# A two-layer decoder on one core: moved feed-forward layers, a reordered junction, and an output projection and bias rows in rounded products

## The reference, cut to what matters

```python
# layer 0, self-attention: ctx is 448 x 2048, out_w is 2048 x 256
return ctx @ out_w + out_b
# layer 0, cross-attention, and layer 1, summary
delta = _nan_clean(ctx @ Wo.T + bo)
proj = jnp.einsum('btd,ed->bte', states, W_out) + b_out
# layer 1, feed-forward: W1 is 1024 x 256, W2 is 256 x 1024, SCALE = 0.1
h = jnp.einsum('bsd,fd->bsf', x, W1)
q = jnp.clip(jnp.round(h / SCALE), -32768, 32767)
return jnp.einsum('bsf,df->bsd', jax.nn.gelu(q * SCALE), W2)
```

## Time and profile before

| quantity | value |
|---|---|
| time, median of 3 runs | 526.32 us (525.9 to 528.05) |
| time of the profiled execution | 528.47 us |
| its span, first to last instruction | 526.7 us |
| around the span | 1.77 us |
| mean granted clock of TensorE | 0.987 |
| TensorE busy | 497.3 us, 94% |
| VectorE busy | 352.1 us, 67% |
| ScalarE busy | 312.9 us, 59% |

### The profile page before, as it was taken

One profiled execution on the slowest core, in us unless ns is written; L12 is line 12 of the kernel. 1 busy time (PEld: TensorE's weight loads), 2 busy tenths in 40 slices (PEclk: granted clock), 3 DMA queues, 4 the chain that ended last, 5 costly groups with the idle time before them and its releaser, 6 DMA issues.

```text
span 526.7 us, 16180 instructions
## 1 busy us (share of the span) xinstructions
PE 497.3 (94%) x7004; PEld 405.7 (77%) x7010; DVE 352.1 (67%) x784; ACT 312.9 (59%) x550; POOL 4.2 (1%) x14
## 2 busy tenths in 40 slices
PE   8999999998889999999999998999999899888897
PEld 7898888886678888877878876888878678645455
DVE  5656767876456764674856686855778764798971
ACT  5657677446256656567566667568467755363252
POOL 1000000000100000000000000000000000000000
PEclk9999999999989999999999999999999999899999
DMA  6366551203202111111211101210111100000000
GB/s 201 110 232 194 189 154 42 60 12 142 88 1 64 59 42 41 41 41 41 75 35 46 27 30 36 67 37 22 40 41 42 51 2 2 1 1 9 1 0 19
DMA packets 12232, 30.84 MB, mean 59 GB/s; under 512 B 1665, under 2 KB 4866, under 8 KB 11394
## 3 DMA queue, kind: packets, MB, share of 16 engines
q1 hardware_dynamic: 11714, 29.07, 17.4%
q0 software_dynamic: 192, 0.51, 0.3%
q10 hardware_dynamic: 256, 0.23, 0.1%
HBM read 29.35 MB, written 0.46 MB: 57 GB/s over the span
## 4 chain that ended last, share of the span: by engine, by line
PE 66%; DVE 17%; ACT 11%; issue 4%; DMA 1%; SPq 0%; DVEq 0%; ACTq 0%
PE psb L1334 10%; PE psb L1324 10%; PE psa L1390 7%; PE psa L1246 6%; PE psb L1408 5%; PE pst L1267 4%; PE psa L1259 3%; PE psb L1297 3%; PE psa L1277 2%; PE pst L1558 2%; ACT shared L590 2%; ACT smem L590 1%; DVE smem L910 1%; PE psb L1288 1%; PE psa L1558 1%
## 5 line engine op out<-in xcount | busy, mean ns | idle before, releaser
L1334 PE MATMUL psb<-wkv,cx 128*125 128x256 f32 x576 | 81.5, 291 | 3.4 <-ACT kx L430 3.4
L1324 PE MATMUL psb<-cx,wkv 128*128 128x500 f32 x276 | 75.4, 409 | 4.1 <-ACT vmem L437 4.1
L1334 PEld LDWEIGHTS psb<-wkv,cx 128*125 128x125 f32 x576 | 72.0, 188 | 7.3 <-ACT kx L430 5.8
L437 ACT ACTIVATE vmem<-psb 125x512 f32<-125x512 f32 x48 | 28.6, 596 | 62.0 <-PE psb L1334 62.0
L1324 PEld LDWEIGHTS psb<-cx,wkv 128*128 128x128 f32 x276 | 48.9, 190 | 16.4 <-ACT vmem L437 4.7
L910 DVE TENSOR_SCALAR shared<-shared,top 125x896 f32<-125x896 f32 x48 | 30.8, 684 | 41.7 <-ACT shared L590 41.5
L1390 PE MATMUL psa<-qb,kx 32*125 32x112 f32 x1536 | 55.6, 282 | 1.4 <-ACT vmem L437 0.8
L1390 PEld LDWEIGHTS psa<-qb,kx 32*125 32x125 f32 x1536 | 47.1, 186 | 9.7 <-issue 4.9
L910 DVE TENSOR_SCALAR smem<-smem,top 125x896 f32<-125x896 f32 x48 | 30.8, 683 | 28.5 <-ACT smem L590 28.5
L590 ACT ACTIVATE shared<-psa 125x1792 f32<-125x1792 f32 x24 | 40.0, 1668 | 13.4 <-PE psa L1390 13.3
L590 ACT ACTIVATE smem<-psa 125x1792 f32<-125x1792 f32 x24 | 40.0, 1666 | 12.0 <-PE psa L1390 11.9
(11 more groups left out here) (311 smaller groups left out, 809.2 us busy)
## 6 DMA issues: line engine op xcount, KB each, us to landing
ring<-ctx_t_dram SPq DMA_DIRECT2D x24, 500.0 KB, 3.4
whd<-wqk_dram SPq DMA_DIRECT2D x16, 256.0 KB, 2.7
qb<-wvp_dram SPq DMA_DIRECT2D x8, 256.0 KB, 3.0
whd<-wo_dram SPq DMA_DIRECT2D x16, 128.0 KB, 2.0
wraw<-w_dram SPq DMA_DIRECT2D x2, 1024.0 KB, 6.0
mats_sb<-mats_dram SPq DMA_DIRECT2D x1, 1536.0 KB, 7.5
wraw<-gate_dram SPq DMA_DIRECT2D x1, 1024.0 KB, 5.0
wraw<-up_dram SPq DMA_DIRECT2D x1, 1024.0 KB, 5.0
```

The costliest lines, as they stand in the source:

```text
L1324: last = nc.tensor.matmul(bank[:, 0:UT], wkv[a][:, 0, c, m * P:(m + 1) * P], cx[b][u % 2][:, c, :], start=(a == b and c == 0), stop=(a == ...
L1334: last = nc.tensor.matmul(bank[0:CT, t * D:(t + 1) * D], cx[b][u % 2][:, c, a0:a0 + CT], wkv[a][:, 1, c, :], start=(a == b and c == 0), st ...
```

## The change

**Output projection.** `output(h)` multiplies split factors: ScalarE rounds the weight (`split_wo`) and the attended values with their bias (`move_oT`, moved from VectorE), VectorE makes the rests (`rest_wo`, `rest_oT`), and six float32r products take the place of two f32 ones. **Bias rows.** Both output biases are split once, at head 13 and 15, and the bias matmul is a float32r product with two rows (-1 times hi, and -1 times the negative rest) in place of an f32 one with one row. **Junction.** `project_vu(0, 0)` is cut in two and `project_k(0, 1)` put behind it; `scores(0)` no longer waits for s_vue. **Feed-forward.** `hidden` of tiles 0 and 1 and `project_hidden(0)` leave the scan for the tail, where `keep_warm` counts are cut; tile 1's second layer goes further down. The clipping of tile 0 is one Relu on ScalarE and one operation on VectorE, that of tile 1 three operations on ScalarE, with gelu scaling by 0.1. Tile 3's layer is handled in quarters. The output rows are written in the order 0, 2, 1, 3.

```diff
 # ScalarE, head loop
+            def split_wo(h):
+                act.wait_ge(s_wo[h % 2], 16 * (h // 2) + 16)
+                if h:
+                    act.wait_ge(s_y, h)
+                nc.scalar.activation(wor[HI][:, :], whd[h % 2][:, QW:QW + D], ACT.Copy).then_inc(s_woh, 1)
+            def move_oT(h):
+                act.wait_ge(s_o, h + 1)
+                nc.scalar.activation(oTr[HI][:, :], PS[2][:, 1, 0:TOK], ACT.Identity, bias=hb[:, h, 2:3]).then_inc(s_oh, 1)
             for h in range(H0):
                 move_pT(h)
+                split_wo(h)
                 if h == 14:
...
                     round_up(0)
+                move_oT(h)
                 if h + 1 < H0:
                     exps(h + 1)
...
+                    act.wait_ge(s_q, 2 * H0)
+                    nc.scalar.activation(minus[:, :], ones[0:2, 0:TT], ACT.Copy, scale=-1.0).then_inc(s_bh, 1)
+                    nc.scalar.activation(bias_hi, single_sb[:, :], ACT.Copy).then_inc(s_bh, 1)
 # VectorE, head loop
-            def move_oT(h):
-                dve.wait_ge(s_o, h + 1)
-                if h:
-                    dve.wait_ge(s_y, h)
-                nc.vector.tensor_scalar_add(oT[:, :], PS[2][:, 1, 0:TOK], hb[:, h, 2:3]).then_inc(s_oe, 1)
+            def rest_wo(h):
+                dve.wait_ge(s_woh, h + 1)
+                nc.vector.tensor_tensor(wor[LO][:, :], whd[h % 2][:, QW:QW + D], wor[HI][:, :].bitcast(F32), ALU.subtract).then_inc(s_wol, 1)
+            def rest_oT(h):
+                dve.wait_ge(s_oh, h + 1)
+                nc.vector.scalar_tensor_tensor(out=oTr[LO][:, :], in0=PS[2][:, 1, 0:TOK], scalar=hb[:, h, 2:3], in1=oTr[HI][:, :].bitcast(F32),
+                                               op0=ALU.add, op1=ALU.subtract).then_inc(s_oe, 1)
...
+                if h == 15:
+                    dve.wait_ge(s_bh, 2)
+                    nc.vector.scalar_tensor_tensor(out=bias2[:, :], in0=bias_hi.bitcast(F32), scalar=ident[0:2, 1:2], in1=single_sb[:, :],
+                                                   op0=ALU.mult, op1=ALU.subtract).then_inc(s_b2, 1)
 # TensorE
             def output(h):
-                pe.wait_ge(s_wo[h % 2], 16 * (h // 2) + 16)
+                pe.wait_ge(s_wol, h + 1)
                 pe.wait_ge(s_oe, h + 1)
                 for m in range(DC):
-                    last = nc.tensor.matmul(pst[:, m, 0:TOK], whd[h % 2][:, QW + m * P:QW + (m + 1) * P], oT[:, :], ...)
+                    for a, b in PARTS:
+                        last = nc.tensor.matmul(pst[:, m, 0:TOK], wor[a][:, m * P:(m + 1) * P], oTr[b][:, :], ...)
...
             output(H0 - 1)
-            project_k(0, 1, A1)
+            project_vu(0, 0, kvb, (0,))
             pe.wait_ge(s_mask, H0)
             turn_y(0)
-            project_vu(0, 0, kvb)
+            project_vu(0, 0, kvb, (1,))
+            project_k(0, 1, A1)
             turn_x1(0)
...
-                if pp == 0:
-                    pe.wait_ge(s_vue, 2)
...
-                nc.tensor.matmul(T0[0:TT, 0:D], ones[0:1, 0:TT], single_sb[0:1, 0, :], start=True, stop=False)
+                nc.tensor.matmul(T0[0:TT, 0:D], minus[:, :], bias2[:, 0:D], start=True, stop=False)
 # TensorE, scan: early(t, o) and late(t, o)
-                if o == 21:
-                    hidden(t, 0)
-                if o == 23:
-                    project_hidden(t)
...
-                if o == 21:
-                    hidden(t, 1)
 # TensorE, tail
             project_out(2)
-            keep_warm(7)
+            hidden(0, 0)
+            keep_warm(4)
             turn_xq(3)
...
-            keep_warm(6)
-            hidden_part(1, 0)
-            keep_warm(6)
+            hidden(0, 1)
+            hidden(1, 0)
+            keep_warm(2)
...
-            hidden_part(1, 1)
+            hidden(1, 1)
...
-            keep_warm(30)
+            keep_warm(12)
+            pe.wait_ge(s_kve, 7)
+            hidden_part(0, 0)
+            hidden_part(0, 1)
+            keep_warm(3)
             turn_x7(2)
...
             hidden_part(2, 0)
             hidden_part(2, 1)
-            keep_warm(22)
+            pe.wait_ge(s_z, 6)
+            hidden_part(1, 0)
+            hidden_part(1, 1)
+            keep_warm(4)
             turn_x7(3)
...
+            for f in range(FC):
+                if f % 2 == 0:
+                    pe.wait_ge(s_hg, 7 + f // 2)
+                last = nc.tensor.matmul(bank_fo[3][0:TT, 0:D], quarter[f // 2][:, (f % 2) * TT:(f % 2 + 1) * TT], w2_sb[:, f, :], ...)
 # ScalarE, tail
             nc.scalar.preload_act_table(ACT.Silu)
+            move_h(0, 0)
             move_xqT(3)
...
-            gelu(1)
             back()
             softmax_exp(2)
+            move_h(0, 1)
+            floor_h(0)
...
+            move_h(1, 0)
...
+            move_h(1, 1)
             move_aT(2)
             root(4, 3)
+            floor_h(1)
...
             move_xbe(3)
+            nc.scalar.activation(hz[1], hz[1], ACT.Relu, bias=low[:, 1:2], scale=-1.0).then_inc(s_zh, 1)
+            nc.scalar.activation(hz[1], hz[1], ACT.Identity, bias=low[:, 2:3], scale=-1.0).then_inc(s_z1, 1)
             move_sy(3)
+            nc.scalar.preload_act_table(ACT.Gelu_apprx_tanh)
+            gelu(0)
+            gelu(1)
+            back()
             softmax_exp(3)
...
+            move_quarter(0)
+            move_quarter(1)
+            gelu_quarter(0)
+            move_quarter(2)
+            gelu_quarter(1)
+            move_quarter(3)
+            gelu_quarter(2)
+            gelu_quarter(3)
 # VectorE, tail
-            last_add(1)
+            nc.vector.tensor_scalar(hz[0], hz[0], 65535.0, -32768.0, ALU.min, ALU.add).then_inc(s_hq, 2)
```

More of the change, by code:

```diff
@@ L81, in decoder @@
         rows_sb = sb("rows_sb", [TT, 4, D])
-        single_sb = sb("single_sb", [1, 2, D])
+        single_sb = sb("single_sb", [2, 2 * D])
+        bias2 = sb("bias2", [2, 2 * D], F32R)
+        bias_hi = cxt[LO][1][0:2, 0:2 * D]
+        minus = sb("minus", [2, TT], F32R)
         cols_sb = sb("cols_sb", [P, 5, DC])
@@ L110, in decoder @@
         yT = xnT
+        wor = [sb(f"wor{k}", [P, D], F32R) for k in range(2)]
+        oTr = [sb(f"oTr{k}", [P, TOK], F32R) for k in range(2)]
         shared = sb("shared", [P, 4, TOK])
@@ L822, in _ @@
                     masked(h + 1)
-                move_oT(h)
+                rest_wo(h)
+                rest_oT(h)
                 if h + 3 < H0:
@@ L1115, in late @@
                     add_normalised(t)
-                if o == 23:
-                    last_add(t)
             for s in range(PAIRS - 2):
@@ L1207, in _ @@
             clip_hidden(2, 1)
+            last_add(0)
             add_proj(3)
@@ L1212, in _ @@
             normalise7(3)
-            clip_hidden(3, 0)
-            clip_hidden(3, 1)
+            last_add(1)
+            for k in range(4):
+                dve.wait_ge(s_z, 7 + k)
+                link(nc.vector.tensor_scalar(quarter[k], quarter[k], MAGIC + 32767.0, MAGIC - 32768.0, ALU.min, ALU.max))
+                nc.vector.tensor_scalar(quarter[k], quarter[k], -MAGIC, 0.1, ALU.add, ALU.mult).then_inc(s_hq, 1)
             last_add(3)
@@ L1326, in project_k, with project_vu @@
                 last.then_inc(s_kp, 1)
-            def project_vu(u, r, bank):
+            def project_vu(u, r, bank, tiles=(0, 1)):
                 pe.wait_ge(s_cx, u + 1)
-                for t in range(2):
+                for t in tiles:
                     a0 = (2 * r + t) * CT
@@ L1335, in project_vu @@
                                                     start=(a == b and c == 0), stop=(a == LO and c == DC - 1))
-                last.then_inc(s_vp, 1)
+                if 1 in tiles:
+                    last.then_inc(s_vp, 1)
             def turn_x1(t):
@@ L1522, in project_out @@
                 pe.wait_ge(s_xbe, 2 * t + 2)
-                nc.tensor.matmul(T1[0:TT, 0:D], ones[0:1, 0:TT], single_sb[0:1, 1, :], start=True, stop=False)
+                nc.tensor.matmul(T1[0:TT, 0:D], minus[:, :], bias2[:, D:2 * D], start=True, stop=False)
                 for c in range(DC):
@@ L1698, in _ @@
             turn_context(3)
-            nc.tensor.matmul(A3[0:TT, 0:D], ones[0:1, 0:TT], single_sb[0:1, 0, :], start=True, stop=False)
+            nc.tensor.matmul(A3[0:TT, 0:D], minus[:, :], bias2[:, 0:D], start=True, stop=False)
             turn_divided(3)
@@ L1753, in _ @@
             keep_warm(2)
-            pe.wait_ge(s_fin, 2)
+            pe.wait_ge(s_z, 4)
             pe.wait_ge(s_xbe, 8)
-            nc.tensor.matmul(A1[0:TT, 0:D], ones[0:1, 0:TT], single_sb[0:1, 1, :], start=True, stop=False)
+            nc.tensor.matmul(A1[0:TT, 0:D], minus[:, :], bias2[:, D:2 * D], start=True, stop=False)
             for c in range(DC):
@@ L1771, in _ @@
             hidden_part(2, 1)
-            keep_warm(22)
+            pe.wait_ge(s_z, 6)
+            hidden_part(1, 0)
+            hidden_part(1, 1)
+            keep_warm(4)
             turn_x7(3)
             keep_warm(1)
```

(18 more changed lines are left out.)

110 lines of the change are left out of this document (54 added, 56 removed).

## The result

The changed kernel took 508.0 us in the median of four executions (507.7 to 511.49) beside 526.46 for the kernel before (525.9 to 528.05, four): a ratio of 0.9663, 95% interval 0.9622 to 0.9704. The forecast was 509.6, its range 505.5 to 513.5. The profiled execution took 511.49 us with a span of 509.7; forecast were 511.8 and 510.0.

A forecast was written before the change was run, and what follows sets the result against it. TensorE, busy 94% of the span, was taken to bound the kernel. Terms 2.2 + 0.75 + 1.75 + 10.6 + 1.4 = 16.7 us gave 511.8 us profiled, 509.6 against the median of 526.32; range 505.5 to 513.5.

The forecast's parts named there:

- Heads: Output projection in the head loop: 0.28 us less a head, nine of fourteen periods winning 0.27; sum 2.2 us.
- Junction: Between heads and scan: scores(0) no longer waits for s_vue, so 0.75 us goes.
- Bias rows and feed-forward layers in the scan: Scan on TensorE: five cheaper bias rows save 1.75 us, feed-forward layers moved out save 10.6 us.
- Tail: After the scan: moved work replaces fillers, and tile 3's second layer directly follows its first; 1.4 us gained.
- rival 2: Junction or tail: the clock falls sooner, around output(14), or in the tail; 512 to 513 us, chance 0.13.
- the likeliest case: Whole kernel: the forecast itself, 509.6 us, with its own range 508 to 511.5; chance 0.50.
- 3: Head loop: ScalarE becomes the bound in most heads, 2.2 turns into nothing or a loss of 1; 512.5 us, chance 0.09.
- 5: Tail: changes of ScalarE's table cost more than their load, making the last softmax late; 512.2 us, chance 0.03.
- 6: Scan: ScalarE or VectorE takes TensorE's place in three steps, half of 10.6 stays; 515 us, chance 0.04.
- 4: Heads: move_oT's wait in ScalarE's list costs each of 15 heads 1.1 us, giving back all 16.7; chance 0.01.
- 1: Behind the junction: the slow clock, costing 2.8 us before, goes; 506.8 us, chance 0.20.

The follow-up runs named there:

- e11: Kernel before with fillers in its junction, at the end of the scan and in the tail; 524.85 us, ratio 0.9970.
- e8: Changed kernel with fillers in the junction and at the end of the scan, and 12 instead of 4 ahead of turn_xq(3); 507.94 us, ratio 0.9651.
- e2: Changed kernel with the bias rows back to one f32 row each, without the operations preparing the rounded ones; 512.3 us, ratio 0.9725.
- e7: Kernel before with the new output projection, bias rows and junction, but layer 1's feed-forward left as before; 522.96 us, ratio 0.9930.
- e10: Kernel before with fillers in its junction alone; 525.86 us, ratio 0.9997.
- e5: Changed kernel with 3 fillers ahead of turn_context(3) and 4 ahead of turn_divided(3); 508.53 us, ratio 0.9673.
- e9: Changed kernel with tile 3's second layer waiting for the last gelu instead of each quarter's own; 511.6 us, ratio 0.9714.

## Why the prediction was right, step by step

By the rows of the table, before against changed, and in brackets with the clock at full in both (e11 against e8):

- Heads, 2.2 foreseen: 2.35 (2.41). Of the thirteen periods up to output(13), by the starts in the timelines, nine shrink by 0.22 to 0.30, 2.5 in all (2.4 foreseen for nine), and the other four grow by 0.02 to 0.08, 0.16 in all (0.2 foreseen). The heavy heads were not quite free, as foreseen.
- Junction, 0.75 foreseen: 1.24 (0.88). The working of the waits was right in what it gains. It carried the clock as a rival, where the clock made the difference: 2.3 us lost (29.80 against 27.46 with fillers), 2.7 won back behind project_q(0) (31.04 against 28.34). Where it says that TensorE had waited three times in 5 us before the fall of the kernel before, the timeline shows two waits there, of 1.32 and 0.54 us.
- Bias rows and feed-forward layers in the scan, 1.75 + 10.6 = 12.35 foreseen: 12.42 (12.24). e2 and e7 split it into 1.60 and 10.89.
- Tail, 1.4 foreseen: 0.99 (1.87). The quarters are worth what they were to be: the second layer starts 1.3 us earlier behind turn_x7(3) than before (1.2 foreseen). This is the one term whose miss has a cause that the step did not name: the stretch of low clock begins 4.3 us behind the last group of weighted values, 1.0 earlier than before (5.3), and slows project_in and project_o (1.44 and 1.91 us), for which VectorE waits. Against the same tails without a stretch it costs 1.6 us (74.39 against 72.81), before 0.7 (75.38 against 74.68), so 0.9 of the gain is lost. What brings the fall forward is not shown; the wait ahead of turn_divided(3) has grown from 0.61 to 0.93 us, which is what the shorter bias row in front of it left over. The prediction had the clock fall in the tail only as part of rival 2.

The sum, 16.7, was 0.3 short of the profiled 17.0 and 0.7 short of the 17.4 at full clock. That the profiled span came so close is luck in part. The forecast had the clock cost both kernels the same. In fact 2.7 us were won and 2.3 lost in the junction, and 0.9 lost in the tail, so that the clock took back 0.5 of the 0.7 by which the terms had been too small. The median of the first set was 1.6 under the forecast, because the forecast moved the profile's clock to the median by the 2.15 us of before, while the changed kernel's timed runs had lost less clock (0.997) than its profile (0.987). On the second chip, at 0.990, the median was 510.0. Both lie in the likeliest case's own range, 508 to 511.5, the first at its very edge.

Of the rivals, 3, 5 and 6 fell to the trace. 4 did not come near. 1 and 2 turned out not to exclude each other or the forecast: in the profile both happened, and how much of the second happens differs from one execution to the next.

## What to carry to other kernels

Where a chain lies wholly on one engine, the price of a part can be summed from its rows to some 0.3 us (scan 12.35 for 12.42, its parts 1.75 for 1.60 and 10.6 for 10.89), and a part undone reads to 0.1 in the trace of that stretch, though the medians of two runs may differ by 2 us for the clock alone. So cut a span at the same instructions in every variant, and put the mean clock beside each time, before a cause is named. When products are moved or shortened, look where TensorE's next longer wait stands and what lies behind it. And fillers in such waits are worth trying, for steadiness more than for time: e10 and e11 moved the kernel before by 0 and 1.35 us.

## What was not expected of the hardware

- One program has its lowered clock at different times in different executions: from 129 to 135.8 us in one profile of the changed kernel, from 127.1 to 130.6 in another, with timed runs between 0.987 and 0.997. Before each such stretch TensorE had stood idle: 1.54 us ahead of output(14) here, 0.82 and 0.93 at the end of the scan, 2.1 for xq(3) in e5. The reverse does not hold: e2 has the wait of 1.54 us and e9 those of 0.82 and 0.93 with the clock at 1.00 behind them.
- The clock costs what stands behind it. At the junction 6.8 us at half clock cost 2.3 us of the changed kernel's time (29.80 against 27.46). In the tail, where VectorE leads, one of 6.8 us cost the kernel before 0.7 (75.38 against 74.68) or, in e10, 0.1 (74.81); one as long cost the changed kernel 1.6 (74.39 against 72.81). In the last it covers project_in and project_o, whose results VectorE waits for; in e10 it begins at 454.1, when project_in is done and most of project_o too.
- Fillers of 512 columns in bfloat16, put where TensorE waits, kept the clock at 1.000 over the whole span: in all six executions of e11 and in two of four of e8.
- An f32 product of a single row and 256 columns costs 0.61 us in the chain; the float32r product of two rows that stands for it costs 0.29.
